# Scattering all eight token tiles of the first batch in one frame of GpSimd's program instead of four in each of two frames

## The reference

```
mod = silu(c) @ wmod                         # six vectors of 256 per batch: sa, ca, ga, sb, cb, gb
h = layernorm(x) * (1 + ca) + sa
x = x + ga' * attention(h)                   # 16 query heads of width 128, 4 key/value heads, causal
h = layernorm(x) * (1 + cb) + sb
x = x + gb' * moe(h)                         # 8 experts of 256x256, the best 2 by gate, softmax weights
```

## Time and profile before

| what | value |
|---|---|
| median of three runs | 909.89 us |
| the profiled execution: its own time | 914.3 us |
| span of that execution (first to last instruction) | 912.1 us |
| PE busy | 877.0 us, 96% of the span |
| DVE busy | 761.5 us, 83% |
| ACT busy | 532.2 us, 58% |
| POOL busy | 321.4 us, 35% |
| one indirect DMA on POOL, median | 960 ns |
| mean granted clock of PE | 0.994 |

### The profile page before, as it was taken

One profiled execution on the slowest core, in us unless ns is written; L12 is line 12 of the kernel. 1 busy time (PEld: TensorE's weight loads), 2 busy tenths in 40 slices (PEclk: granted clock), 3 DMA queues, 4 the chain that ended last, 5 costly groups with the idle time before them and its releaser, 6 DMA issues.

```text
span 912.1 us, 16758 instructions
## 1 busy us (share of the span) xinstructions
PE 877.0 (96%) x5337; PEld 769.0 (84%) x5337; DVE 761.5 (83%) x1725; ACT 532.2 (58%) x1223; POOL 321.4 (35%) x395
## 2 busy tenths in 40 slices
PE   5899999999999999999999999999999999898996
PEld 4788888888888888888888998888888888787774
DVE  5777888888888888878788888888889897678798
ACT  4487666666666666663766666666666665444321
POOL 3464222222222222141624444444322225417685
PEclk9999999999999999999999999999999999899999
DMA  7000400000000000300000000000000004342122
GB/s 242 7 12 13 145 13 13 12 12 12 12 12 12 12 12 13 105 12 1 16 9 13 13 13 13 12 13 13 12 13 13 13 13 141 116 166 96 57 81 82
DMA packets 31845, 36.12 MB, mean 40 GB/s; under 512 B 2506, under 2 KB 29428, under 8 KB 31604
## 3 DMA queue, kind: packets, MB, share of 16 engines
q1 hardware_dynamic: 30180, 31.08, 10.5%
q0 software_dynamic: 1536, 4.20, 1.4%
q10 hardware_dynamic: 64, 0.02, 0.0%
HBM read 28.08 MB, written 10.22 MB: 42 GB/s over the span
## 4 chain that ended last, share of the span: by engine, by line
PE 85%; DVE 8%; issue 2%; ACT 2%; DMA 1%; another core or an unknown queue 0%; POOL 0%; SPq 0%; DVEq 0%; ACTq 0%; POOLq 0%
PE ps_t L898 13%; PE ps_s L787 8%; PE ps_s L791 8%; PE ps_s L788 8%; PE ps_o L779 7%; PE ps_o L783 7%; PE ps_o L780 7%; PE ps_m L787 3%; PE ps_m L791 3%; PE ps_m L788 3%; PE ps_m L779 3%; PE ps_m L783 3%; PE ps_m L780 3%; PE ps_o L908 2%; ACT probs L1283 1%
## 5 line engine op out<-in xcount | busy, mean ns | idle before, releaser
L1233 ACT ACTIVATE pt_hi<-ps_t 128x512 fp32r<-128x512 f32 (+2 forms) x320 | 170.9, 534 | 130.1 <-PE ps_t L898 122.2
L1283 ACT ACTIVATE probs<-ps_s,neg_max 128x128 f32<-128x128 f32 (+7 forms) x256 | 189.9, 742 | 79.2 <-DVE neg_max L1636 76.4
L1645 DVE TENSOR_TENSOR pt_lo<-ps_t,pt_hi 128x512 fp32r<-128x512 f32 (+2 forms) x320 | 192.1, 601 | 16.0 <-ACT pt_hi L1233 12.2
L1636 DVE TENSOR_REDUCE neg_max<-ps_s 128x1 f32<-128x128 f32 (+7 forms) x256 | 192.3, 751 | 3.7
L898 PE MATMUL ps_t<-ident,probs 128*128 128x128 f32 x1152 | 189.0, 273 | 0.9 <-DVE pt_lo L1645 0.9
L591 POOL TENSOR_TENSOR q_lo<-raw,q_hi 128x512 fp32r<-128x512 f32 x60 | 77.4, 1290 | 318.4 <-ACT q_hi L1233 318.4
L898 PEld LDWEIGHTS ps_t<-ident,probs 128*128 128x128 f32 x1152 | 142.1, 141 | 20.8 <-DVE pt_lo L1645 4.9
L787 PE MATMUL ps_s<-k_hi,q_hi 128*128 128x512 f32 (+2 forms) x354 | 148.6, 420 | 3.8 <-ACT probs L1283 3.8
L1683 DVE SCALAR_TENSOR_TENSOR acc<-ps_m,rsum,acc 128x256 f32<-128x256 f32 x256 | 111.3, 476 | 17.6 <-PE ps_m L791 16.8
L1630 DVE TENSOR_TENSOR ps_s<-ps_s,mask 128x128 f32<-128x128 f32 x256 | 75.4, 295 | 59.1 <-PE ps_s L791 51.9
L791 PE MATMUL ps_s<-k_hi,q_lo 128*128 128x512 f32 (+2 forms) x354 | 123.4, 349 | 0.0
(11 more groups left out here) (244 smaller groups left out, 1704.7 us busy)
## 6 DMA issues: line engine op xcount, KB each, us to landing
wq_raw<-in_L_attn_wq_dram SPq DMA_DIRECT2D x32, 128.0 KB, 2.3
wo_raw<-in_L_attn_wo_dram SPq DMA_DIRECT2D x32, 128.0 KB
slot_out_dram<-y_slot SPq DMA_DIRECT2D x23, 128.0 KB, 1.7
slot_rows<-slot_rows_dram SPq DMA_DIRECT2D x2, 1280.0 KB, 10.7
wkv_raw<-in_L_attn_wkv_dram SPq DMA_DIRECT2D x2, 1024.0 KB, 6.7
x_again<-in_L_attn_x_dram SPq DMA_DIRECT2D x2, 1024.0 KB, 5.9
we_raw<-in_L_ffn_expert_w_dram SPq DMA_DIRECT2D x1, 2048.0 KB, 8.3
acc<-in_L_attn_x_dram SPq DMA_DIRECT2D x2, 512.0 KB, 4.5
```

The costliest lines, as they stand in the source:

```text
L1233: return nc.scalar.activation(dst, src, ACT.Copy, scale=scale)
L1283: nc.scalar.activation(probs[par][:, prob_offset(i):prob_offset(i) + w], ps_s[:, i % 2, col:col + w], ACT.Exp, bias=neg_max[:, par, i:i + ...
L1636: nc.vector.tensor_reduce(neg_max[:, par, i:i + 1], ps_s[:, i % 2, col:col + w], AXIS_X, ALU.max, negate=True).then_inc(max_set, 1)
L1645: nc.vector.tensor_tensor(pt_lo[:, q % PT, lo:CH], ps_t[:, q % 2, lo:CH], pt_hi[:, q % PT, lo:CH].bitcast(F32), ALU.subtract).then_inc(pt_ ...
```

## The change

The tuple that names the frames with scatters has one entry instead of two. With it `per` is 8 instead of 4, so that frame 13 calls `scatter_rows` for token tiles 0 to 7 and frame 14 calls it for none. Nothing else is changed.

```diff
--- before.py
+++ after.py
@@ -107,7 +107,7 @@
 FIRST_ROUTED = 1
 CHOOSE_FRAME = 10
 RANK_FRAME = 12
-SCATTER_FRAMES = (13, 14)
+SCATTER_FRAMES = (13,)
```

## The result

The changed kernel takes 919.94 us (median of four runs, 918.37 to 922.57) against 909.07 us for the kernel before (908.21 to 910.55). The ratio is 1.0121, with a 95% interval of 1.009 to 1.0151: 10.9 us slower. Run again beside the kernel before on chip 3 it was 918.43 against 909.54 us, ratio 1.0106 (1.0089 to 1.0123). On which chip the first comparison and the first recording of the kernel before ran isn't on record. The recorded execution of the change took 920.99 us with a span of 918.8.

What follows compares the result with a forecast made beforehand. PE, busy 96% of the span, was taken to bound the kernel. Profiled 914.3 + 7.9 + 2.3 - 4.6 = 919.9 us; median 909.9 + 9.55 + 2.3 = 921.7; forecast 920.5 between them, range 914.0 to 925.5 us.

Steps and rivals of the forecast that it cites:

- The eight more scatters: Frame 13, POOL: `q_lo` queued behind sixteen issues 1.265 us apart, ending at 778.13; PE stands 7.9 us at L791.
- the second sum: Timed runs without late PE signals: 909.9 + 9.55 us stall at L791 + 2.3 for the half clock = 921.7 us.
- held signals: PE's signals delayed toward a burst's end, released when over; ACT's first copies in frames 14, 15 idle 2.94, 4.33 us.
- The clock: After the L791 stall PE's clock falls to 0.50 for 3.5 to 5.9 us, costing 2.3 us (1.7 to 2.95).
- No scatters in frame 14: Start of frame 15: 3.1 us won at L954 plus 1.5 for the clock, 4.6 us together (0 to 6.1).
- SP's list: SP issues `x_again` earlier, the slot table still waits for the last scores; 4.9 us of cover left, cost nothing.
- How it stands to the median: Profiled execution took 4.4 us more than the median; forecast 920.5 us, between 919.9 and 921.7.
- the view behind it: Late PE signals exist only while an execution is recorded; timed runs lack them, so frame 15 has nothing to win.
- The one at 919.9: Sum against the profiled execution: 914.3 + 7.9 (stall) + 2.3 (clock) - 4.6 (frame 15) = 919.9 us.
- in every run: Rival, chance 0.25: timed runs have the late PE signals too, so the whole sum applies: 909.9 + 5.6 = 915.5 us.
- The slower burst: Rival, chance 0.14: scatters 9 to 16 beside the 2 MB weight load delay `q_lo` up to 4.1 us; 924.6 us.
- The burst that fits: Rival, chance 0.05: later scatters cost less than 1.265 us, break-even at 0.86; at least spacing 905.5 us.

Runs made afterwards that it cites:

- filler kernel: Kernel before, with 22 POOL tensor_scalar operations and no added DMA between frame 13's eight scatters and `q_lo`: 921.97 us, ratio 1.0075.

## Why the prediction was right

The forecast was 920.5 us, the measured median 919.94; the recorded execution was put at 919.9 us and took 920.99, with 1.6 us of that from the half clock near the kernel's start.

*The eight more scatters.* Right, in place and size. Spacing 1.268 us for 1.265, `q_lo` at once behind the last, L791 as the instruction that stands, 7.96 us later than before for the 7.9 of the sum. The idle time itself is 9.47 us, as in the second sum (9.55), since this recording has no held signals that would delay PE first. The filler kernel, the kernel with `q_lo` on DVE on chip 0, and the stalls of ten and twelve scatters each show it apart.

*The clock.* Right: 2.41 us for 2.3, and 1.9 on chip 3 (from L791 to the first transposes of frame 15 it took 19.81 us there, and 17.87 in the kernel before). PE worked 5.3 us at 0.50 after the stall (779.77 to about 785.1), inside the bounds of 3.5 and 5.9 us; with twelve scatters it was 2.8 us, outside them. The Trainium skill's page "TensorE: Matmul & The Clock Gate", section "Part 1: The HAM clock gate (the "warmup" mystery)", has these two levels and lets an idle PE fall to the lower; the trace agrees, with 0.50 behind stalls of 2.33, 3.80, 4.31 and 9.47 us and 1.00 behind 1.81.

*No scatters in frame 14.* This term of 4.6 us did not act in the comparison that was forecast. Laid over the first recording it seems to come out (3.28 us at L954 for the 3.1, and 2.1 behind it for the 1.5), but that recording has held signals and the recording of the change has none. Without held signals no run shows anything to win: with ten scatters in frame 13 and six in frame 14, on chip 3, PE idles 0.52 us at L954 as well. With them there is: on chip 5 PE idles 2.33 us at this step with eight and eight scatters, and this with all sixteen in frame 13 and `q_lo` on DVE:

```profile
801.75 0.44 PE L954 MATMUL ps_t<-ident,spread 128*128 128x128 f32 x2 [0.51 <-DVE pt_lo L1645]
```

That is 1.8 us won at L954 and 1.4 behind it (18.56 against 17.17 us to the first L981), 3.2 for the 4.6.

*SP's list.* Right: `x_again` moved up (779.88 for 791.97), the slot table still waited for the last scores (799.75), and PE had no idle time at the first L981.

*How it stands to the median.* The number was right and the view behind it was not, and that it came within 0.6 us is in part luck. 920.5 lies between two sums. The one at 919.9 takes off the 4.6 us that weren't there to win. The one at 921.7 has the right terms for a place without held signals, and is too high: stall and clock are 9.47 + 2.41 = 11.9 us, the measured loss is 10.9. On chip 3 they are 9.36 + 1.94 = 11.3, and the loss is 8.9. About 0.9 us of that is won behind the first L981: against the kernel with the second burst moved, the change is 11.28 us later there and 10.4 at the end (916.2 against 905.8). The rest stays open.

The view itself: I took the gap between the recorded 914.3 us and the median of 909.9 as a sign that held signals exist only while an execution is recorded, and read the Trainium skill's page "NOTIFIC — the notification-queue block" in that way. The runs speak against it. On chip 5 the kernel before takes 913.65 us in its timed runs, and signals are late in all four recordings; on chips 3 and 0 it takes 909.54 and 908.90 us, and none of seven recordings shows a late signal. On chip 4 it takes 912.40 us, and no burst of eight was recorded. The first recording, at 914.3 us, may come from another chip than the runs at 909.07. Each chip was used in one stretch of time only, so whether the held signals go with the chip or with the time isn't separated. The rival "in every run" (915.5 us) fits chip 5 as to the kernel before. Its price for the change, 5.6 us over the kernel before, is untested, since the change was not run on chip 5 or 4. I had overlooked that a long burst holds PE's signals for long by itself: on chip 5 the kernel with free `q_lo` and sixteen scatters lost 6.9 us, and the one with the filler 8.3. Whether an execution that nothing records has held signals stays open: each of the timed runs reports a span and a clock too.

*The rivals.* The slower burst: sixteen issues beside a DMA share of 0.84 and more kept their spacing, so it is out. The burst that fits: out, by the same spacing.

## What to carry to other kernels

An engine that computes little but issues DMAs is a queue: count everything behind the issues in its list, and its distance to the instruction that waits. Here 0.7 us of slack stood against 10.1 us of issues, and the stall went by the issue. A half clock came on top behind the stalls of 2.33 us and more, and not behind 1.81. Put such issues in small groups behind whatever the bound engine needs next, and time a kernel on more than one chip before a difference of half a per cent is explained.

## What was not expected of the hardware

PE's signals to ACT, DVE and SP can arrive late during and behind a burst of indirect DMAs. This is seen in the first recording of the kernel before and in all four recordings on chip 5, and in none of the seven on chips 3 and 0. In the first recording ACT's copies started 2.1 and 3.3 us behind the end of PE's transposes. On chip 5 the held signals of two bursts of eight cost 4.6 us (1.39, 1.81 and 1.39, above). On chip 4, where the kernel before takes 912.40 us, bursts of four save 3.9; that the cause is the same there isn't shown by a recording.

With sixteen scatters in one burst, on chip 5, DVE waited 7.14 us for scores that PE had finished, and went on 1.1 us after the last issue. The release isn't tied to the end of the burst: in the same recording ACT's copy started at 770.55 and SP's load at 776.89, both before the burst was over, and with all sixteen in frame 14 a copy started at 792.81 in a burst that ended at 800.15. ACT and DVE signalled each other without delay in the same stretch (in the kernel with `q_lo` on DVE, DVE's mask and maximum at 779.00 and 779.34 and ACT's exponential at 779.66 follow at once). What holds the signals, and why only in some places, isn't settled. Loads issued by SP, at a DMA share of 0.97, left PE busy for 2.00 of 2.00 us.
